# Products of zeros on TensorE before the first score products and between them

## The reference

```
qkv  = x @ qkv_w.T + qkv_b                       # 16 heads of 8
attn = softmax(q k^T * 8**-0.5) @ v              # per batch and head, 512 x 512 scores
x1   = layernorm(x + (attn @ fc_w.T + fc_b + x))
h    = silu((x1 @ w1.T) * w1_s) * ((x1 @ w2.T) * w2_s)    # 128 -> 512
h    = gelu((h @ h1.T) * h1_s)                            # 512 -> 512
h    = gelu((h @ h2.T) * h2_s)                            # 512 -> 512
out  = layernorm(x1 + (h @ w3.T) * w3_s)                  # 512 -> 128
```

## Time and profile before

| | us |
|---|---|
| median of three runs | 323.35 |
| lowest, highest | 321.71, 323.61 |
| the profiled execution's own time | 322.21 |
| its span in the profile | 320.4 |
| PE busy | 295.8 (92%) |
| DVE busy | 244.1 (76%) |
| ACT busy | 234.8 (73%) |
| POOL busy | 148.8 (46%) |
| mean granted TensorE clock | 0.965 of full speed |

### The profile page before, as it was taken

One profiled execution on the slowest core, in us unless ns is written; L12 is line 12 of the kernel. 1 busy time (PEld: TensorE's weight loads), 2 busy tenths in 40 slices (PEclk: granted clock), 3 DMA queues, 4 the chain that ended last, 5 costly groups with the idle time before them and its releaser, 6 DMA issues.

```text
span 320.4 us, 5569 instructions
## 1 busy us (share of the span) xinstructions
PE 295.8 (92%) x1804; PEld 138.5 (43%) x1804; DVE 244.1 (76%) x516; ACT 234.8 (73%) x433; POOL 148.8 (46%) x227
## 2 busy tenths in 40 slices
PE   8567998999997999999999999999999999999991
PEld 6421132422332344334544233625634353579990
DVE  3959899998989899998996859298684410289883
ACT  3562567999683896898688998697799989447340
POOL 6762038651043793118807778063478913610201
PEclk9985899999999899999999999999999999999996
DMA  5643353313211321212030023310100010000101
GB/s 151 184 92 54 58 192 88 55 24 51 35 19 18 68 36 16 42 22 43 0 57 29 6 47 48 71 20 0 33 4 2 2 33 0 4 0 2 33 2 38
DMA packets 17830, 13.44 MB, mean 42 GB/s; under 512 B 2551, under 2 KB 16648, under 8 KB 17800
## 3 DMA queue, kind: packets, MB, share of 16 engines
q1 hardware_dynamic: 17546, 12.85, 19.2%
q10 hardware_dynamic: 254, 0.20, 0.2%
HBM read 5.51 MB, written 1.05 MB: 20 GB/s over the span
## 4 chain that ended last, share of the span: by engine, by line
PE 60%; ACT 11%; DVE 9%; POOL 8%; issue 6%; DMA 4%; SPq 1%; ACTq 1%; POOLq 0%; DVEq 0%
PE bank L445 26%; PE bank L480 11%; PE bank L465 9%; PE bank L456 6%; DVE negmax L803 6%; ACT prob L654 4%; DMA h_nat<-in_L_ffn_h_w_dram 3%; PE bank L420 2%; ACT L654 2%; POOL hT L990 2%; POOL parts L960 2%; PE bank L531 1%; ACT h_nat L729 1%; PE bank L438 1%; PE bank L503 1%
## 5 line engine op out<-in xcount | busy, mean ns | idle before, releaser
L803 DVE TENSOR_REDUCE negmax<-bank 128x1 f32<-128x512 f32 x256 | 160.2, 682 | 23.0 <-PE bank L456 22.5
L654 ACT ACTIVATE prob<-bank 128x512 f32<-128x512 f32 x256 | 136.7, 604 | 29.0 <-PE bank L465 27.4
L480 PE MATMUL bank<-prob,v_sb 128*32 128x512 f32 x512 | 73.0, 608 | 0.4 <-ACT prob L654 0.3
L456 PE MATMUL bank<-stack 61*128 61x512 bf16 x256 | 65.9, 398 | 4.3 <-DMA stack<-parts 2.6
L445 PE MATMUL bank<-act,hT 128*128 128x512 f32 (+1 forms) x320 | 68.3, 359 | 0.1
L465 PE MATMUL bank<-stack 64*128 64x512 bf16 x256 | 61.4, 389 | 2.2 <-DVE negmax L803 1.0
L445 PEld LDWEIGHTS bank<-act,hT 128*128 128x128 f32 x320 | 49.2, 190 | 14.3 <-issue 6.4
L722 ACT ACTIVATE h_nat<-bank,hs_all 128x512 f32<-128x512 f32 (+1 forms) x40 | 22.8, 603 | 22.4 <-PE bank L445 22.4
L456 PEld LDWEIGHTS bank<-stack 61*128 61x128 bf16 x256 | 17.6, 94 | 49.7 <-issue 26.9
L978 POOL CAST mparts<-negmax 128x16 bf16<-128x16 f32 (+1 forms) x17 | 3.7, 219 | 74.3 <-DVE negmax L803 74.3
L465 PEld LDWEIGHTS bank<-stack 64*128 64x128 bf16 x256 | 14.0, 94 | 51.0 <-issue 36.2
(11 more groups left out here) (120 smaller groups left out, 343.0 us busy)
## 6 DMA issues: line engine op xcount, KB each, us to landing
stack<-parts SPq DMA_DIRECT2D x124, 48.0 KB
x_in<-in_L_attn_x_dram SPq DMA_DIRECT2D x4, 256.0 KB, 4.7
h_nat<-in_L_ffn_h_w_dram SPq DMA_DIRECT2D x1, 1024.0 KB, 8.1
work<-in_L_ffn_h_w_dram SPq DMA_DIRECT2D x1, 1024.0 KB, 5.6
res<-in_L_attn_x_dram SPq DMA_DIRECT2D x4, 256.0 KB, 2.9
out_dram<-y SPq DMA_DIRECT2D x3, 256.0 KB, 2.3
work<-in_L_ffn_w_w_dram SPq DMA_DIRECT2D x2, 256.0 KB, 3.0
stack<-mT SPq DMA_DIRECT2D x30, 6.0 KB
```

Of the source, the lines that this page charges most:

```text
L456: nc.tensor.matmul(space("S", n)[:, :], stack[0][half_of(h, MROW), h // 2, qt * P:(qt + 1) * P], stack[1][half_of(h, MROW), h // 2, :], st ...
L480: last = nc.tensor.matmul(space("P", pfirst)[at:at + VW, :], v_sb[b % 2][:, kt, of:of + VW], prob[:, t % NP, :], start=kt == 0 and slot % ...
L654: nc.scalar.activation(prob[:, n % NP, :], space("T", n)[:, :], ACT.Exp, scale=SCALE).then_inc(emptied("T", n), 1)
L803: nc.vector.tensor_reduce(negmax[:, g % 2, col:col + 1], space("S", n)[:, :], AX.X, ALU.max, negate=True).then_inc(emptied("S", n), 1)
```

## The change

It adds 66 products of `wz` with itself to TensorE's list, all before the first T step; nothing is removed and no bank of another step changes. One K (four products) into bank 7 stands ahead of `v:0`, seven K into bank 4 stand between `v:0` and the first S. A new kind of step, Z, is K with two products; 17 of them stand among the 21 S steps: ahead of each S from the fifth on, except that the last Z of one group stands ahead of `m`.

```diff
-x:0 wq:1 q:2 q:3 v:4 wt:5 wt:6 wt:0 wt:1 wt:2 wt:3 x:5 wf:6 v:0 S:5 S:4 S:6 S:0 S:1 S:2 S:5 S:4 S:3 S:6 S:0 S:1 S:2 S:5 m:4 S:3 S:6 S:0 S:4 S:1 S:2
+x:0 wq:1 q:2 q:3 v:4 wt:5 wt:6 wt:0 wt:1 wt:2 wt:3 x:5 wf:6 K:7 v:0 K:4*7 S:5 S:4 S:6 S:0 Z:1 S:1 Z:2 S:2 Z:5 S:5 Z:3 S:4 Z:3 S:3 Z:0 S:6 Z:0 S:0 Z:1
+S:1 Z:2 S:2 Z:4 S:5 Z:3 m:4 S:3 Z:0 S:6 Z:0 S:0 Z:1 S:4 Z:1 S:1 Z:2 S:2 Z:3 S:5 T:3 T:6 T:0 m:4 S:1 S:3 S:4 T:2 P:7 S:6 S:0 T:5 T:2 S:1 P S:3 S:4 T:5
...
@@ -612,6 +612,9 @@
                 elif what == "K":
                     until_free(pe, "K", n)
                     keep_busy(4, space("K", n)).then_inc(emptied("K", n), 1)
+                elif what == "Z":
+                    until_free(pe, "Z", n)
+                    keep_busy(2, space("Z", n)).then_inc(emptied("Z", n), 1)
```

More of the change, by code:

```diff
@@ L13 @@
 PE_ORDER = """
-x:0 wq:1 q:2 q:3 v:4 wt:5 wt:6 wt:0 wt:1 wt:2 wt:3 x:5 wf:6 v:0 S:5 S:4 S:6 S:0 S:1 S:2 S:5 S:4 S:3 S:6 S:0 S:1 S:2 S:5 m:4 S:3 S:6 S:0 S:4 S:1 S:2
-S:5 T:3 T:6 T:0 m:4 S:1 S:3 S:4 T:2 P:7 S:6 S:0 T:5 T:2 S:1 P S:3 S:4 T:5 T:6 S:2 P S:0 S:1 T:5 T:6 P T:3 S:4 T:5 T:2 S:6 P S:0 S:1 T:3 T:5 S:4 S:2
-m:6 P T:0 S:3 S:6 S:1 q:5 S:4 S:0 q:2 x:3 T:6 T:1 P T:5 T:3 S:4 S:6 T:2 P T:1 T:5 S:0 S:3 S:4 hs:2 P T:1 T:6 T:5 S:2 wt:0 S:1 T:3 P S:6 T:4 T:0 S:2
-S:5 S:1 m:3 S:4 T:6 P T:0 T:3 S:2 S:6 S:5 wt:1 wt:0 wt:4 wt:3 S:2 S:1 S:6 S:0 T:5 T:4 P T:3 T:2 T:5 S:1 S:4 S:6 o:0 T:1 S:3 S:4 T:2 S:6 P:7 T:0 S:5
@@ L18 @@
[L18 to L33, removed]
@@ L34 @@
-H*9 H:4157 H*9 W:3 W*3 K:0 W:2 W Y:0 W K:1 W K:0 Y:6
+x:0 wq:1 q:2 q:3 v:4 wt:5 wt:6 wt:0 wt:1 wt:2 wt:3 x:5 wf:6 K:7 v:0 K:4*7 S:5 S:4 S:6 S:0 Z:1 S:1 Z:2 S:2 Z:5 S:5 Z:3 S:4 Z:3 S:3 Z:0 S:6 Z:0 S:0 Z:1
+S:1 Z:2 S:2 Z:4 S:5 Z:3 m:4 S:3 Z:0 S:6 Z:0 S:0 Z:1 S:4 Z:1 S:1 Z:2 S:2 Z:3 S:5 T:3 T:6 T:0 m:4 S:1 S:3 S:4 T:2 P:7 S:6 S:0 T:5 T:2 S:1 P S:3 S:4 T:5
+T:6 S:2 P S:0 S:1 T:5 T:6 P T:3 S:4 T:5 T:2 S:6 P S:0 S:1 T:3 T:5 S:4 S:2 m:6 P T:0 S:3 S:6 S:1 q:5 S:4 S:0 q:2 x:3 T:6 T:1 P T:5 T:3 S:4 S:6 T:2 P
@@ new lines @@
+T:1 T:5 S:0 S:3 S:4 hs:2 P T:1 T:6 T:5 S:2 wt:0 S:1 T:3 P S:6 T:4 T:0 S:2 S:5 S:1 m:3 S:4 T:6 P T:0 T:3 S:2 S:6 S:5 wt:1 wt:0 wt:4 wt:3 S:2 S:1 S:6
+S:0 T:5 T:4 P T:3 T:2 T:5 S:1 S:4 S:6 o:0 T:1 S:3 S:4 T:2 S:6 P:7 T:0 S:5 T:3 m:4 S:1 T:6 S:2 T:0 S:5 P T:4 S:1 S:2 T:3 S:6 T:5 S:0 T:1 L:4 T:2 S:3 P
+T:5 T:6 T:4 S:1 S:0 S:2 P T:3 T:5 T:1 S:6 S:0 S:4 T:2 P T:3 T:6 T:5 S:1 S:0 S:2 T:4 P T:3 T:6 T:1 S:5 S:0 S:4 m:2 T:3 P T:5 S:6 S:2 S:0 S:1 P S:4 S:3
+v:5 o:6 T:2 T:0 T:1 S:4 T:5 S:2 T:3 S:0 T:1 S:4 a:6 T:5 T:3 S:2 T:1 S:0 f:6 q:4 q:5 T:2 T:3 T:1 S:6 S:0 P:7 T:4 T:2 S:6 S:3 P T:1 T:0 S:4 S:2 P S:6
@@ new lines @@
+S:1 m:3 x:0 P S:5 X:4 S:3 S:0 S:2 T:6 T:1 A:4 B:6 T:5 T:1 T:3 S:0 S:6 S:2 T:5 m:4 T:1 P T:0 T:3 T:4 S:6 S:5 S:2 A:1 B:0 T:6 T:3 P S:5 S:2 T:0 S:4 A:1
+B:6 T:5 T:3 T:0 S:2 P S:4 S:6 T:2 S:5 A:1 B:3 T:4 S:0 T:2 T:6 P S:5 S:3 S:0 S:4 H:1 H o:2 H S:5 S:6 S:3 T:0 P:7 T:4 S:2 S:0 T:5 H m:6 H:4 H S:3 T:5
+T:6 T:2 S:1 S:0 H*2 S:5 S:3 T:6 T:1 T:2 S:0 P S:4 S:5 T:6 T:1 T:3 S:2 P S:0 S:4 T:6 T:1 T:5 S:3 P T:2 S:6 S:0 T:1 T:4 S:5 m:3 H:2 H S:6 T:1 T:3 T:0
+S:4 S:5 H*2 T:1 S:6 T:3 T:4 S:0 S:5 H:2 H T:6 S:1 S:3 T:0 T:4 S:5 H*2 S:6 S:1 T:0 T:3 T:4 S:5 P S:2 S:6 S:0 S:1 m:5 P S:2 S:6 P S:0 S:1 P T:5 T:2 T:3
@@ new lines @@
+S:6 S:4 v:0 o:1 q:5 q:6 a:2 T:4 T:3 T:0 S:1 S:5 P:7 T:2 T:6 S:4 S:1 T:3 S:0 f:5 H:2 H T:4 T:6 S:3 S:5 H*2 m:4 H:6 H*2 T:1 T:2 T:4 S:0 H H:3 H T:1 T:5
+S:2 S:0 S:6 T:4 H X:1 H T:5 T:2 T:4 S:0 P S:3 S:6 T:5 S:1 S:0 A:2 B:3 A:4 B:5 A:6 S:1 S:3 S:0 T:2 P T:5 T:4 T:1 B:2 A:6 B:5 H:3 T:4 T:0 T:1 H*3 T:2
+S:6 S:4 S:5 P S:3 S:6 m:4 P S:5 S:3 P S:6 S:5 P T:4 T:3 S:0 S:6 S:1 T:5 T:2 W:4 T:0 S:3 T:6 S:5 P T:2 T:1 T:0 S:3 W o:6 W T:5 T:2 S:3 T:1 P:7 T:0 T:6
+W m:5 T:3 T:2 S:1 S:0 P Y:6 S:4 T:5 T:1 T:3 S:0 S:2 P T:6 T:5 T:4 H:1 H T:3 T:0 S:6 S:5 H T:2 T:4 S:3 S:6 T:0 P T:5 T:2 T:4 H H:3 H*3 T:0 T:6 T:5 S:2
@@ new lines @@
+S:1 S:4 H:3 H*3 H:0 H*3 T:2 T:6 T:1 S:5 S:4 S:3 P S:0 S:5 P S:4 S:3 P S:0 S:5 m:4 P S:3 S:2 S:4 S:0 T:6 T:5 o:1 T:3 T:6 P:7 T:2 T:5 a:3 S:4 T:1 T:6
+S:0 S:2 P S:5 T:4 T:3 S:1 T:0 S:6 f:2 H:4 H*2 T:5 T:3 T:1 S:0 S:2 S:6 H H:5 H*3 H:3 S:0 S:4 T:1 T:2 T:6 S:5 H*3 H:1 H*3 m:2 X:0 S:6 T:4 T:3 T:5 S:1
+S:2 P S:6 A:0 P S:1 S:2 S:6 P S:1 S:2 T:4 T:0 B:3 W:6 A:5 B:4 S:1 T:3 T:2 T:0 W P T:3 T:1 S:4 T:5 A:2 B:0 A:3 B:4 m:1 W*2 T:5 T:2 T:1 P Y:3 T:0 P T:6
+T:5 T:4 H:2 o:3 T:1 T:0 P:7 T:6 T:5 T:4 P T:3 T:1 H T:0 T:6 H T:5 T:4 P T:3 T:1 T:0 H H:6 H*3 T:5 T:4 T:3 H:1 H*3 T:2 T:0 T:6 H:5 H*3 T:4 T:3 T:1 P
@@ L35 @@
+T:2 P*2 K:0*5 T:0 P T:6 K:1*2 P K:0*2 o:5 K:0*2 a:4 a:3 K:0 f:1 H:2 H*3 H:0 H*3 f:6 H:7 H*3 H:5 H*3 X:4 K:0 X:3 W:1 W A:2 B:0 A:6 B:7 A:5 B:4 A:2 B:3
+A:6 B:0 A:5 B:7 A:2 B:4 A:6 B:5 W*2 H:3206 H*4 Y:7 H*5 H:4157 H*9 H:3206 H*9 H:4157 H*9 W:3 W*3 K:0 W:2 W Y:0 W K:1 W K:0 Y:6
 """
```

## The result

The changed kernel takes 328.67 us (median of four runs, 327.65 to 330.53) against 323.48 us before (four runs, 321.71 to 324.94): ratio 1.0169, 95% interval 1.0101 to 1.0238. It is slower by 5.2 us where 0.8 us less was forecast. The profiled execution took 330.53 us, its span is 328.7 us.

A forecast was written before the change was run, and what follows sets the result against it. DVE's maxima bound the kernel to 31.55 us, then TensorE, at half clock until 35.1 us. -1.22 us for full clock and +0.41 for the K steps gave -0.8: 322.7 - 0.8 = 321.9 us, range 320.4 to 324.0.

The forecast's parts named there:

- If it stays full through 32 us: Condition on the granted clock under which TensorE's work from 31.59 us gets 1.22 us shorter.
- Z among the S: price 0: Seventeen Z among the score products: 9.7 us at full clock against DVE's 10.2 us, so DVE hides them.
- The zeros make TensorE the bound: Rival, chance 0.13: clock falls early, near 21 to 25 us, DVE runs dry; +0.4 to +3.5 us, middle +1.7.
- The half-clock tile: Score tile with its Z at half clock: 0.98 us on TensorE, 0.75 in the others, against DVE's 0.60.
- the bound of +3 us: Seventeen Z tiles at half clock throughout: about 15 us, less 10.2 and some 2 us of tiles in advance.
- K steps: Seven K ahead of the first S, 0.457 us each, put DVE's second maximum at 21.09 us: +0.41 us.
- The gain at full clock: TensorE's P, S and T steps from 31.59 us run at full clock: -1.22 us.
- DVE's cap: DVE idles 1.43 us between 34.5 and 42 us; less 0.41, 1.0 us is the most the change can gain.
- A Z at full clock: Score tile whose S waits for its Z's bank: 0.665 us, 0.06 more than DVE needs.
- The rule against it: Short idle times between product groups as banks cycle can make the clock go to and fro; then none of 1.22 us.

The follow-up runs named there:

- e2: The change with its eight K steps left out, only the seventeen Z of two products each: ratio 1.0212 to the kernel before.
- e9: The change with four products in each Z instead of two, all bank waits kept: ratio 1.0044 to the kernel before.
- e3: The change with each Z's two products put into a bank nobody reads, without waiting or raising a counter: ratio 1.0070 to the kernel before.
- e5: The change with each Z cut to one product of a single column, all bank waits kept: ratio 1.0111 to the kernel before.
- e1: The change with every Z removed, only the eight K steps of four products each: ratio 1.0037 to the kernel before.
- e6: The change without Z, its K replaced by unwaiting zeros, 24 products ahead of the first S and 20 before the second: ratio 0.9987 to the kernel before.
- e4: The change with four products in each Z, into a bank nobody reads, without waiting or raising a counter: ratio 0.9992 to the kernel before.
- e8: e6 plus four free zeros as each Z and 48 free zero products in the pause near 9.6 us: ratio 0.9952 to the kernel before.
- e10: e8 plus three waiting groups of six zero products in TensorE's pauses ahead of the first feed-forward product: ratio 1.0021 to the kernel before.
- e11: The kernel before with only 48 free zero products added in the pause near 9.6 us: ratio 0.9979 to the kernel before.
- e13: e8 with three free zeros a tile instead of four: 322.50 us against 324.60 for the kernel before, ratio 0.9940.
- e14: The whole change plus 48 free zero products in the pause near 9.6 us: ratio 1.0093 to the kernel before.

## Why the prediction was wrong

The step that failed is the condition of the clock: "If it stays full through 32 us". It did not; it fell at 26.3 us. With it fell "Z among the S: price 0", whose cover was DVE's 0.60 us a tile.

- *The mechanism was in the rivals, with 0.13 and too small.* "The zeros make TensorE the bound" is what happened. The half-clock tile was put at 0.98 us and 0.75 without a wait; it measures 0.99 and 0.87. Its middle of +1.7 us took the clock to be half for only a part of the Z stretch, and part 1 measures +4.1. Even the bound of +3 us "if the clock stays down throughout" was too low: e2, whose 17 Z all ran at half clock, has +6.8. There the tiles took 16.0 us (22.27 to 38.29) and not 15. The three T steps and the m between the 21st and the 22nd S took another 1.4 us, which DVE had hidden before and which the sum left out. And the 2 us of tiles in advance spared nothing, since TensorE's own list had become the longer one. The second term was missing as well: the low stretch reached 5.8 us into TensorE's own work instead of 3.5, so that part 2 lost another 1.1 us instead of nothing. The range ended at 324.0 us because it held the lower half of this rival only.
- *The chance was wrong for a reason that the profile showed.* I asked only whether the pause ahead of the scores was filled. But in the kernel before the clock had not risen through 10.1 us in which TensorE had 7.93 us of busy records, so a list paced by DVE does not raise it of itself. Two waiting zeros a tile did not hold it and four did, with the same waits (the change and e9).
- *K steps: right in mechanism.* They fill 18.39 to 21.45 us, 0.46 us a step; the first S came at once behind them. The forecast +0.41 us on DVE's start shows in e3 and e5, which have the same K steps and no half clock ahead of the scores: their second maximum comes at 20.63 + 0.60 = 21.2 and 20.53 + 0.60 = 21.1 us, some 0.5 us behind the 20.68 of before. That price was right. What was missed is that putting the fall off can move the low stretch onto work that pays for it (e1, part 2 +0.6). It need not: e6's fell at 25.0 us as well, but ended at 35.2, as before, and its part 2 is +0.3.
- *The gain at full clock: right.* -1.22 us was the sum and 1.43 us DVE's cap; the runs with a full clock give -1.3 and -1.5 us in part 2. The prize was real and of the forecast size; the change did not win it.
- *A Z at full clock: nearly right.* 0.665 us forecast, 0.67 measured. It hid behind DVE while the clock was full.
- *The rule against it* (the Trainium skill, TensorE: Matmul & The Clock Gate, section "A second HAM failure mode: psum-queue depth-cycling") fits the change in part: its clock fell amid short pauses between groups, but only once, and it rose once. It would not have told e9 apart, which has the same bank cycling and the same waits and kept the full clock.

## What to carry to other kernels

Filler on an engine is free only while the engine's list, at its slow clock, is still shorter than the one that paces it; price filler at the slow clock first, and if it doesn't fit there, either make it enough to hold the clock or leave it out. Filler must not wait: a bank that nobody reads and no counter made the same zeros 0.5 to 1% cheaper (e9 against e4; the change against e3, where the clock also fell later). And see where a low stretch lies: what DVE covered, before the 22nd S, cost nothing (10.1 us of it in the kernel before), and behind it every us cost about 0.4, 1.3 us before and 2.8 in e3.

## What the runs showed of the hardware

- With two waiting zeros a tile the clock fell to 1.2 GHz at 26.3 us, with four and the same waits it stayed at 2.4 GHz from 20 to 50 us; with free ones it fell at 32.0 us with two and not in that stretch with three or four. The ratios were 1.0169, 1.0044, 1.0070, 0.9947 and 0.9992.
- The clock can be half from 12 to 19 us as well (12.6 to 16.0 after, 14.9 to 18.3 in e1, none before), behind the idle pause from about 10 us. Of the eleven profiles without zeros in that pause seven show it, of the five with them (e8, e10, e11, e13, e14) none. The length of the pause does not tell which: after 2.67 us idle the clock fell (after), after 3.44 us it did not (before). Where it is low, the maxima start late: the second one comes at 21.95 to 24.04 us in those seven, at 20.16 to 21.92 in the other nine.
- Mean granted clock is a poor measure of the gain: e8 has 0.987 against 0.965 and is 0.5% faster.
